# First attention of a fused decoder layer: sums from a column of ones, outputs normalised token by token

## The chip, the core and the metric

The kernel runs on one core of one Trainium2 chip. The metric is the device time of one execution in microseconds. The core has the engines PE (TensorE: matmuls and weight loads), DVE (VectorE), ACT (ScalarE), POOL (GpSimd) and SP (SyncE, which issues the transfers here). Each engine works through its own list of instructions in order; they wait for one another by semaphores.

## The reference, cut to what matters

Sixteen sequences of 512 tokens with 256 channels run through two blocks. The first is attention with 16 heads of 16 channels, whose part that is changed here reads as follows (`x` has been normalised, `q` and `k` are normalised per head):

```python
scores = jnp.einsum('nhld,nhmd->nhlm', q, k) * SM_SCALE
scores = jnp.where(causal, scores, NEG)
attn = jax.nn.softmax(scores, axis=-1)
out = jnp.einsum('nhlm,nhmd->nhld', attn, v)
out = out.transpose(0, 2, 1, 3).reshape(N, L, EMB)
return out @ Wo.T + bo
```

The second block is another causal attention with a small latent (16 heads, 32 value channels shared between the heads) and a mixture of eight experts beside a shared one. Everything is float32. Products with weights are made of three matmuls, high by high, high by low and low by high, where "high" is the operand rounded to the matmul's type fp32r and "low" the remainder (`TERMS` in the kernel).

## The kernel before

The 16 sequences ("batches") are worked on one after the other, with loops on every engine that wait for each other's signals. A batch takes some 250 us: projections and the first attention, projections and the second attention, the experts. Both attentions run through the same functions, with `a` 0 for the first and 1 for the second.

An attention has 16 units, `u`. A unit is one group of four heads, `g = u // 4`, and one tile of 128 tokens, `tile_of(u) = u % 4`. By the causal mask tile j needs keys of j+1 blocks of 128. Per unit:

1. PE makes the scores of the four heads into four PSUM banks (`score`, lines 608 and 614, the second adds the mask). The scores of unit u+1 stand in front of what PE does for unit u; each head's score waits for the exponential of the same head in the unit before.
2. DVE takes the maximum of each row, head by head (line 1055).
3. ACT makes the exponentials (line 839) into `prob` and accumulates their row sums into `sums`, which appears in the trace as an ACTIVATION_READ_ACCUMULATOR behind each one.
4. PE transposes `prob` block by block (line 625) into two PSUM banks by turns. DVE (line 1063) or ACT (line 810) copies each block to `probt`: of the ten blocks of a group ACT has the third, sixth and ninth.
5. PE multiplies the transposed blocks with the values (`weigh_values`, line 636) and adds up the output of a group in PSUM bank 6, the four heads below one another, 32 rows each, with only 16 of them filled in the first attention (`va` has zeros in the others). `weigh_values(u - 1)` stands behind the first blocks of unit u.

When a group is through, its outputs are divided by the sums: DVE takes the reciprocal (line 1067), POOL spreads it over the 32 columns of a head (`rexp`, line 459), PE transposes that (line 645) into PSUM bank 7, ACT copies bank 6 to `osb` (line 810), DVE multiplies the two to `onm` (line 1074), ACT rounds it (`oth`) and POOL, for the last group DVE, subtracts (`otl`, lines 464 and 1093). For group g this is spread over the following group: PE's transposes stand in unit 4g+4, ACT's copy and DVE's product in unit 4g+5, ACT's rounding in 4g+6. At the end of an attention PE makes the output product, for each of four token tiles over four groups of 128 rows, of which 64 are zeros in the first attention (`project_out`, line 677), and DVE adds it to the residual (line 1100).

What sets the order is the order written in each engine's `attend` function. The kernel functions that the change touches follow with their line numbers.

Of the kernel before, what the change touches and what calls it, by code (L numbers as in the profile page):

```python
# [99 lines left out]
def _build(nc, ctx, dram):  # L100
# [20 lines left out]
    woa = new("woa", [P, 2, NG, C], F32R)  # L121
# [29 lines left out]
    sums = new("sums", [P, 2, UNITS, G], F32)  # L151
    rsum = new("rsum", [P, 2, UNITS, G], F32)
# [22 lines left out]
    place[0] += 4096  # L175
    oth = at("oth", [P, NG, L], F32R, region_x)
# [33 lines left out]
    onm = new("onm", [P, L], F32)  # L210
    rexp = new("rexp", [P, NT, G, HP], F32)
# [5 lines left out]
    r_woa = new("r_woa", [P, NG, C], F32)  # L217
# [23 lines left out]
    zeroed = sem("zeroed")  # L241
# [57 lines left out]
    rsum_ready = Signal(sem("rsum_ready"), 2 * NG)  # L299
    rexp_ready = Signal(sem("rexp_ready"), 2 * NG)  # L300
    rsumt_psum = Signal(sem("rsumt_psum"), 2 * NG)
    osb_ready = Signal(sem("osb_ready"), 2 * NG)
    onm_ready = Signal(sem("onm_ready"), 2 * NG)
    oth_ready = Signal(sem("oth_ready"), 2 * NG)
    otl_ready = Signal(sem("otl_ready"), 2 * NG)
# [74 lines left out]
    def _(sp):  # L380
# [58 lines left out]
    def _(pool):  # L439
        chain = Chain(pool, pool_link, POOL_LINKS)  # L440
        nc.gpsimd.memset(r_woa[:, :, :], 0.0).then_inc(zeroed, 1)
# [4 lines left out]
        pool.wait_ge(va_zeroed, 1)  # L446

# [20 lines left out]
        def sequence(b, last):  # L468
# [26 lines left out]
            spread_sums(b, 0)  # L495

# [25 lines left out]
            spread_sums(b, 1)  # L522
# [11 lines left out]
    def _(pe):  # L534
# [14 lines left out]
        pe.wait_ge(va_zeroed, 1)  # L549
# [256 lines left out]
    def _(act):  # L806
# [25 lines left out]
        def exps(b, a, u, part):  # L832
# [474 lines left out]
```

## Time and profile before

| | us |
|---|---|
| median of 3 runs (lowest, highest) | 4082.11 (4074.95, 4089.76) |
| profiled execution | 4099.86 |
| its span, first to last instruction | 4098.0 |
| PE busy | 3508.8 (86%) |
| DVE busy | 3057.7 (75%) |
| ACT busy | 2302.6 (56%) |
| POOL busy | 805.5 (20%) |
| mean granted TensorE clock | 0.924 of 2.4 GHz |

The busy time of an engine is the time in which it works on an instruction. Every row that is shown further down has times in microseconds unless it says ns. Matmuls overlap, so the interval from one row to the next tells their pace better than their duration. A bracket at the end of a row of the timeline is the time for which the engine sat idle before it, and what released it. The granted clock is 1.00 at 2.4 GHz and 0.50 at 1.2 GHz.

### The profile page before, as it was taken

The numbers are of one execution on the slowest core, as the hardware profiler recorded it, in microseconds if no ns is written. First come the engines' busy times: TensorE is split into PE (matmuls) and PEld (weight loads), VectorE is DVE, ScalarE is ACT, GpSimd is POOL, SyncE is SP. The second block draws the span as 40 slices with busy tenths as digits, with TensorE's granted clock in tenths as the row PEclk, the third lists the DMA queues.
The fourth block names the chain that finished last, engine by engine and source line by source line (L and its number), as shares of the span: only waits on it lengthen the run. The fifth ranks groups of instructions, "written<-read, shape, count | busy, mean of one in ns | idle before, by whom it ended". The sixth has DMA issues, their size and how long they took to land.

```text
span 4098.0 us, 93072 instructions
## 1 busy us (share of the span) xinstructions
PE 3508.8 (86%) x31392; PEld 2764.5 (67%) x31392; DVE 3057.7 (75%) x6444; ACT 2302.6 (56%) x6346; POOL 805.5 (20%) x951
## 2 busy tenths in 40 slices
PE   3898888989889898897988989888898888989888
PEld 2676766767667676676766767667676766767667
DVE  3778777687777877778777687877878777787776
ACT  2655546565465654646646466554656546565464
POOL 1212222022220222202222122221212222022220
PEclk9899999999999998999989989999999999999999
DMA  3000000000000000000000000000000000000000
GB/s 73 7 2 7 7 7 7 2 7 7 7 7 2 7 7 7 7 1 12 2 7 7 7 7 2 7 7 7 7 2 7 7 7 7 2 7 7 6 2 6
DMA packets 33906, 30.35 MB, mean 7 GB/s; under 512 B 8864, under 2 KB 33312, under 8 KB 33376
## 3 DMA queue, kind: packets, MB, share of 16 engines
q1 hardware_dynamic: 33376, 23.68, 2.0%
q8 instruction: 284, 4.65, 0.5%
q14 instruction: 246, 2.02, 0.2%
HBM read 15.28 MB, written 8.39 MB: 6 GB/s over the span
## 4 chain that ended last, share of the span: by engine, by line
PE 57%; issue 14%; DVE 12%; ACT 10%; POOL 5%; SPq 1%; ACTq 0%; DVEq 0%; DMA 0%; POOLq 0%
PE bank L625 12%; PE scores L723 9%; ACT prob L839 6%; PE bank L636 6%; PE scores L612 6%; PE bank L735 4%; PE scores L613 4%; PE scores L614 3%; PE bank L596 2%; POOL qf L503 2%; PE scores L697 2%; PE scores L608 2%; PE scores L677 2%; DVE negmax L1055 1%; PE bank L555 1%
## 5 line engine op out<-in xcount | busy, mean ns | idle before, releaser
L839 ACT ACTIVATE prob<-scores,negmax 128x128 f32<-128x128 f32 (+3 forms) x2048 | 1060.7, 538 | 221.8 <-DVE negmax L1055 178.6
L1055 DVE TENSOR_REDUCE negmax<-scores 128x1 f32<-128x128 f32 (+3 forms) x2048 | 885.4, 484 | 101.0 <-PE scores L614 87.6
L625 PE MATMUL bank<-ident,prob 128*128 128x128 f32 x5120 | 730.8, 280 | 44.9 <-DVE probt L1063 35.6
L1063 DVE COPY probt<-bank 128x512 f32<-128x512 f32 x896 | 597.5, 685 | 179.2 <-PE bank L625 172.2
L625 PEld LDWEIGHTS bank<-ident,prob 128*128 128x128 f32 x5120 | 548.2, 142 | 156.0 <-DVE probt L1063 66.3
L614 PE MATMUL scores<-mask,ident 128*128 128x128 bf16 x2048 | 450.0, 231 | 0.0
L612 PE MATMUL scores<-khh,qt 128*128 128x256 f32 (+2 forms) x1024 | 438.4, 429 | 13.3 <-ACT qt L810 7.5
L839 ACT ACTIVATION_READ_ACCUMULATOR prob<-scores,negmax 128x1 f32 x2048 | 437.6, 214 | 0.0
L810 ACT ACTIVATE probt<-bank 128x512 f32<-128x512 f32 x384 | 233.0, 607 | 205.6 <-PE bank L625 205.6
L613 PE MATMUL scores<-kll,qt 128*128 128x256 f32 (+2 forms) x1024 | 345.4, 337 | 0.0
L596 PE MATMUL bank<-ident,stk 128*128 128x128 bf16 x2048 | 203.8, 286 | 153.2 <-DVE stk L1153 122.2
L723 PE MATMUL scores<-xth,wgu 128*128 128x512 f32 x1152 | 329.6, 409 | 0.0
L608 PE MATMUL scores<-qkt 96*128 96x128 bf16 (+3 forms) x1024 | 266.4, 306 | 45.9 <-DVE qkt L1043 13.9
L596 PEld LDWEIGHTS bank<-ident,stk 128*128 128x128 bf16 x2048 | 184.0, 133 | 173.2 <-issue 121.3
L614 PEld LDWEIGHTS scores<-mask,ident 128*128 128x128 bf16 x2048 | 205.2, 100 | 140.8 <-issue 110.4
L464 POOL TENSOR_TENSOR otl<-onm,oth 128x512 fp32r<-128x512 f32 x96 | 122.5, 1276 | 897.0 <-ACT oth L810 897.0
L459 POOL COPY rexp<-rsum 128x512 f32<-128x512 f32 x128 | 78.3, 612 | 856.2 <-DVE rsum L1067 856.2
L723 PEld LDWEIGHTS scores<-xth,wgu 128*128 128x128 f32 x1152 | 215.1, 195 | 44.0
L960 ACT ACTIVATE sg<-scores 128x512 f32<-128x512 f32 x144 | 86.3, 599 | 280.3 <-PE scores L723 280.3
L451 POOL TENSOR_TENSOR rstd<-var,expo 128x4 f32<-128x4 f32 x64 | 67.0, 1053 | 897.9 <-DVE var L1115 551.6
L735 PE MATMUL bank<-wd,hidh 128*128 128x256 f32 x1152 | 212.0, 281 | 27.1 <-ACT hidh L810 21.8
L612 PEld LDWEIGHTS scores<-khh,qt 128*128 128x128 f32 x1024 | 220.7, 216 | 17.7 <-ACT qt L810 9.3
(179 smaller groups left out, 6967.4 us busy)
## 6 DMA issues: line engine op xcount, KB each, us to landing
x_in<-in_x_rows SPq DMA_DIRECT2D x16, 512.0 KB, 3.5
out_rows<-x SPq DMA_DIRECT2D x16, 512.0 KB, 3.6
r_gu<-in_wg SPq DMA_DIRECT2D x2, 512.0 KB, 5.0
r_gu<-in_wu SPq DMA_DIRECT2D x2, 512.0 KB, 5.5
r_d<-in_wd SPq DMA_DIRECT2D x1, 1024.0 KB, 6.8
r_wqt<-in_wq_nope_t SPq DMA_DIRECT2D x1, 512.0 KB, 6.2
r_wqr<-in_wq SPq DMA_DIRECT2D x2, 256.0 KB, 8.8
r_wob<-in_wo SPq DMA_DIRECT2D x1, 512.0 KB, 5.3
```

What stands on the lines that cost most here:

```text
L596: ins = nc.tensor.transpose(out[:, i * P:(i + 1) * P], stk[:, t % 2, quad * 8 + i].rearrange("p s d -> p (s d)"), ident16[:, :])
L608: mm(bank[q][:, 0:n], qkt[:, h, j * P:(j + 1) * P], qkt[:, H + h, 0:n], start=True, stop=False)
L612: mm(bank[q][:, 0:m], tok, khh[:, 0:m], start=True, stop=False)
L613: mm(bank[q][:, 0:m], tok, kll[:, 0:m], start=False, stop=False)
L614: ins = mm(bank[q][:, n - P:n], ident16[:, :], mask16[:, :], start=False, stop=True)
L625: ins = nc.tensor.transpose(bank[4 + n % 2][:, q * P:(q + 1) * P], prob[:, u % 2, q, i * P:(i + 1) * P], ident[:, :])
L636: ins = mm(bank[6][q * HP:(q + 1) * HP, j * P:(j + 1) * P], val, probt[:, u % 2, i, q * P:(q + 1) * P], start=i == 0, stop=i == j)
L723: ins = mm(bank[2 * s + w][:, :], wgu[:, w_, e, k, w * I:(w + 1) * I], XT[x_][:, k], start=m == 0 and k == 0, stop=m == 2 and k == KC - 1)
L735: ins = mm(bank[4 + 2 * s + t // 2][:, (t % 2) * C:(t % 2 + 1) * C], (hidh, hidl)[x_][:, s, t * P:(t + 1) * P], wd[:, w_, e], start=m == 0 ...
L839: nc.scalar.activation(prob[:, u % 2, q, 0:n], bank[q][:, 0:n], ACT.Exp, bias=negmax[:, a, u, q:q + 1], accum_out=sums[:, a, u, q:q + 1]). ...
L1055: nc.vector.tensor_reduce(negmax[:, a, u, M * part:M * part + M], scores[:, M * part:M * part + M, 0:n], axis=AX.X, op=ALU.max, negate=Tru ...
L1063: nc.vector.tensor_copy(probt[:, u % 2, i], bank[4 + n % 2][:, :]).then_inc(probt_dve.sem, 1)
```

## The change

In the first attention only, the sum of a row of exponentials no longer comes from ACT's accumulator. The values `va` get a one in column 16 of each head's 32, so that `weigh_values` also yields the row sums, in row 16 of the head's 32 rows of bank 6. ACT copies bank 6 to `osb` as before. PE transposes `osb` (`transpose_out`), which gives 128 tokens by 128 columns per tile in bank 7. DVE takes the reciprocals of column 16 of every head and multiplies the 16 output columns by them, per token (`normalise_first`), into `otok`, where the 256 channels stand without gaps. When two groups are there, PE transposes `otok` back (`transpose_tok`), ACT rounds (`split_first`) and DVE subtracts (`low_first`), and the output product runs over two full blocks of 128 rows instead of four half-filled ones (`project_first`). POOL has no part in it any more. The output weight `woa` has two blocks instead of four and is loaded in one piece.

```diff
         nc.gpsimd.memset(va[:, :, :, :], 0.0).then_inc(va_zeroed, 1)
         pool.wait_ge(va_zeroed, 1)
+        nc.gpsimd.memset(va[:, :, :, D], 1.0).then_inc(va_zeroed, 1)
+        pool.wait_ge(va_zeroed, 2)
...
-        sp.wait_ge(zeroed, 1)
-        for q in range(G):
-            load(r_woa[q * HP:q * HP + D],
-                 dram["wo1t"].rearrange("(g q d) n -> q d g n", q=G, d=D)[q])
+        load(r_woa[:, :, :], dram["wo1t"].rearrange("(k p) n -> p k n", p=P))
...
-            spread_sums(b, 0)
...
+        def transpose_out(b, g):
+            pe.wait_ge(osb_ready.sem, osb_ready.at(b, g + 1))
             if g > 0:
-                pe.wait_ge(onm_ready.sem, onm_ready.at(b, a * NG + g))
+                pe.wait_ge(otok_ready.sem, otok_ready.at(b, g))
+            if g == NG - 2:
+                pe.wait_ge(o1l_ready.sem, o1l_ready.at(b, 1))
+            for j in range(NT):
+                ins = nc.tensor.transpose(bank[7][:, j * P:(j + 1) * P], osb[:, j * P:(j + 1) * P], ident[:, :])
+            ins.then_inc(outt_psum.sem, 1)
+
+        def transpose_tok(b, k):
+            pe.wait_ge(otok_ready.sem, otok_ready.at(b, 2 * k + 2))
+            for t in range(NT):
+                ins = nc.tensor.transpose(bank[7][:, t * P:(t + 1) * P], otok[:, t, k * P:(k + 1) * P], ident[:, :])
+            ins.then_inc(o1_psum.sem, 1)
+
+        def project_first(b, k):
+            for t in range(NT):
+                if t == 0:
+                    pe.wait_ge(o1h_ready.sem, o1h_ready.at(b, k + 1))
+                    pe.wait_ge(o1l_ready.sem, o1l_ready.at(b, k + 1))
+                for m, (x_, w_) in enumerate(TERMS):
+                    ins = mm(bank[t][:, 0:C], (o1h, o1l)[x_][:, k, t * P:(t + 1) * P], woa[:, w_, k],
+                             start=m == 0 and k == 0, stop=m == 2 and k == KC - 1)
+                if k == KC - 1:
+                    ins.then_inc(y_psum.sem, 1)
...
                 transpose_prob(b, a, u, range(early))
                 if u > 0:
                     weigh_values(b, a, u - 1)
-                    if u % NT == 0:
-                        transpose_sums(b, a, u // NT - 1)
+                    if a == 1 and u % NT == 0:
+                        transpose_sums(b, u // NT - 1)
+                    if a == 0 and u % NT == 2 and u > NT:
+                        transpose_out(b, u // NT - 1)
+                    if a == 0 and u == 3 * NT:
+                        transpose_tok(b, 0)
                 transpose_prob(b, a, u, range(early, tile_of(u) + 1))
-            transpose_sums(b, a, NG - 1)
+            if a == 1:
+                transpose_sums(b, NG - 1)
             weigh_values(b, a, UNITS - 1)
-
-            project_out(b, a, range(NG - 2))
-            project_out(b, a, range(NG - 2, NG))
...
+            if a == 0:
+                project_first(b, 0)
+                transpose_out(b, NG - 1)
+                transpose_tok(b, 1)
+                project_first(b, 1)
+            else:
+                project_out(b, range(NG - 2))
+                project_out(b, range(NG - 2, NG))
...
+                row_sums = {"accum_out": sums[:, u, q:q + 1]} if a == 1 else {}
                 nc.scalar.activation(prob[:, u % 2, q, 0:n], bank[q][:, 0:n], ACT.Exp, bias=negmax[:, a, u, q:q + 1],
-                                     accum_out=sums[:, a, u, q:q + 1]).then_inc(prob_ready.sem, 1)
+                                     **row_sums).then_inc(prob_ready.sem, 1)
...
+        def split_first(b, k):
+            act.wait_ge(o1_psum.sem, o1_psum.at(b, k + 1))
+            copy(o1h[:, k], bank[7][:, :]).then_inc(o1h_ready.sem, 1)
...
-                if u % NT == 2 and u > NT:
-                    split_out(b, a, u // NT - 1)
+                if a == 1 and u % NT == 2 and u > NT:
+                    split_out(b, u // NT - 1)
+                if a == 0 and u == 3 * NT:
+                    split_first(b, 0)
             copy_out(b, a, NG - 1)
-            split_out(b, a, NG - 1)
+            if a == 0:
+                split_first(b, 1)
+            else:
+                split_out(b, NG - 1)
...
+        def normalise_first(b, g):
+            dve.wait_ge(outt_psum.sem, outt_psum.at(b, g + 1))
+            out = bank[7].rearrange("p (t h d) -> p t h d", t=NT, h=G)
+            nc.vector.reciprocal(rs1[:, :, :], out[:, :, :, D]).then_inc(rs1_ready.sem, 1)
+            dve.wait_ge(rs1_ready.sem, rs1_ready.at(b, g + 1))
+            tt(otok[:, :, g * G * D:(g + 1) * G * D].rearrange("p t (h d) -> p t h d", h=G), out[:, :, :, 0:D],
+               rs1[:, :, :].unsqueeze(3).to_broadcast([P, NT, G, D]), ALU.mult).then_inc(otok_ready.sem, 1)
+
+        def low_first(b, k):
+            dve.wait_ge(o1h_ready.sem, o1h_ready.at(b, k + 1))
+            tt(o1l[:, k], bank[7][:, :], o1h[:, k].bitcast(F32), ALU.subtract).then_inc(o1l_ready.sem, 1)
...
-                if u > 0 and u % NT == 0:
-                    invert_sums(b, a, u // NT - 1)
+                if a == 1 and u > 0 and u % NT == 0:
+                    invert_sums(b, u // NT - 1)
                 for i in mine:
                     copy_block(b, a, u - 1, i)
-                if u % NT == 1 and u > NT:
-                    normalise_out(b, a, u // NT - 1)
-
-            normalise_out(b, a, NG - 1)
-            dve.wait_ge(oth_ready.sem, oth_ready.at(b, (a + 1) * NG))
+                if a == 1 and u % NT == 1 and u > NT:
+                    normalise_out(b, u // NT - 1)
+                if a == 0 and u % NT == 2 and u > NT:
+                    normalise_first(b, u // NT - 1)
+                if a == 0 and u == 3 * NT:
+                    low_first(b, 0)
+            if a == 0:
+                normalise_first(b, NG - 1)
+                low_first(b, 1)
+                return
```

DVE's list before, in unit 5 of the first attention (`negmax` are the maxima, `probt` a block's copy, `onm` the product with the spread reciprocals):

```order
159 L1055 TENSOR_REDUCE negmax<-scores 128x1
160 L1060 REGISTER_ALU
161 L1062 REGISTER_ALU
162 L1063 COPY probt<-bank 128x512
163 L1070 ISA
164 L1074 TENSOR_TENSOR onm<-bank,osb 128x512
165 L1054 REGISTER_ALU
166 L1055 TENSOR_REDUCE negmax<-scores 128x1
```

The product stands behind the maxima of unit 5 and in front of those of unit 6. DVE's list of the changed kernel, in unit 6, between the maxima of unit 6 and those of unit 7:

```order
169 L1108 TENSOR_REDUCE negmax<-scores 128x1
170 L1113 REGISTER_ALU
171 L1115 REGISTER_ALU
172 L1116 COPY probt<-bank 128x512
173 L1125 RECIPROCAL rs_129<-bank 128x16
174 L1127 TENSOR_TENSOR otok<-bank,rs_129 128x4x64
175 L1107 REGISTER_ALU
176 L1108 TENSOR_REDUCE negmax<-scores 128x1
```

A reciprocal and a product that read PSUM bank 7 stand there now, one unit later than the product did. PE's list of the changed kernel at the same place (the last two scores of unit 7, a block of unit 6, the values of unit 5, the transposes of `osb`, the other blocks of unit 6, a score of unit 8):

```order
163 L619 MATMUL scores<-mask_59,ident_58 128x128
164 L611 REGISTER_ALU
165 L613 MATMUL scores<-qkt 128x512
166 L619 MATMUL scores<-mask_59,ident_58 128x128
167 L628 REGISTER_ALU
168 L630 MATMUL bank<-ident,prob 128x128 x4
169 L641 MATMUL bank<-probt,va 32x128 x4
170 L638 REGISTER_ALU
171 L641 MATMUL bank<-probt,va 32x128 x4
172 L652 MATMUL bank<-ident,osb 128x128 x4
173 L630 MATMUL bank<-ident,prob 128x128 x4
174 L628 REGISTER_ALU
```

PE's list before, in unit 4, where the transposes of the spread reciprocals stood:

```order
137 L636 MATMUL bank<-probt,va 32x128 x12
138 L633 REGISTER_ALU
139 L636 MATMUL bank<-probt,va 32x128 x4
140 L645 MATMUL bank<-ident,rexp 128x128 x4
141 L606 REGISTER_ALU
142 L608 MATMUL scores<-qkt 128x384
143 L614 MATMUL scores<-mask_59,ident_58 128x128
```

PE's transposes for a group's outputs moved from unit 4g+4, in front of the scores of unit 4g+6, to unit 4g+6, behind the scores of unit 4g+7.

## Rows read from the trace of the kernel before

**Rows 1.** Page: busy us, share, instructions; and a costly group with its mean ns.
```profile
PE 3508.8 (86%) x31392; PEld 2764.5 (67%) x31392; DVE 3057.7 (75%) x6444; ACT 2302.6 (56%) x6346; POOL 805.5 (20%) x951
L839 ACT ACTIVATION_READ_ACCUMULATOR prob<-scores,negmax 128x1 f32 x2048 | 437.6, 214 | 0.0
```

**Rows 2.** Busy times by stretch: length, PE, PEld, DVE, ACT, POOL, clock, DMA, GB/s.
```profile
2156.54:2169.80 13.26, 12.31 (x160) 8.83 (x157) 11.78 (x26) 11.07 (x38) 1.88 (x2) 1.00 0.01 1
```

**Rows 3.** Timeline of DVE, units 8 to 12: start, duration, instruction, idle before.
```profile
2156.54 0.99 DVE L1055 TENSOR_REDUCE negmax<-scores 128x1 f32<-128x128 f32 x4 [0.27 <-PE scores L614]
2157.45 0.24 DVE L1067 RECIPROCAL rsum<-sums 128x16 f32<-128x16 f32 x1
2157.78 1.29 DVE L1063 COPY probt<-bank 128x512 f32<-128x512 f32 x2
2159.94 0.69 DVE L1063 COPY probt<-bank 128x512 f32<-128x512 f32 x1 [0.88 <-PE bank L625]
2160.55 1.41 DVE L1055 TENSOR_REDUCE negmax<-scores 128x1 f32<-128x256 f32 x4
2161.88 0.68 DVE L1063 COPY probt<-bank 128x512 f32<-128x512 f32 x1
2162.80 0.69 DVE L1074 TENSOR_TENSOR onm<-bank,osb 128x512 f32<-128x512 f32 x1 [0.24 <-PE bank L645]
2163.40 1.94 DVE L1055 TENSOR_REDUCE negmax<-scores 128x1 f32<-128x384 f32 x4
2165.86 2.48 DVE L1055 TENSOR_REDUCE negmax<-scores 128x1 f32<-128x512 f32 x4
2169.80 0.98 DVE L1055 TENSOR_REDUCE negmax<-scores 128x1 f32<-128x128 f32 x4 [0.27 <-PE scores L614]
```

**Rows 4.** Timeline of PE, units 8 to 11.
```profile
2161.97 0.66 PE L645 MATMUL bank<-ident,rexp 128*128 128x128 f32 x4
2164.35 1.09 PE L625 MATMUL bank<-ident,prob 128*128 128x128 f32 x8
2165.28 0.38 PE L608 MATMUL scores<-qkt 96*128 96x512 bf16 x1
...
2165.56 0.38 PE L608 MATMUL scores<-qkt 96*128 96x512 bf16 x1
...
2166.76 0.60 PE L625 MATMUL bank<-ident,prob 128*128 128x128 f32 x4
2167.30 0.65 PE L636 MATMUL bank<-probt,va 128*32 128x128 f32 x16
...
2168.99 0.66 PE L625 MATMUL bank<-ident,prob 128*128 128x128 f32 x4 [0.46 <-DVE probt L1063]
```

**Rows 5.** Timeline of DVE and PE, end of the first attention.
```profile
2188.59 0.69 DVE L1074 TENSOR_TENSOR onm<-bank,osb 128x512 f32<-128x512 f32 x1 [1.47 <-ACT osb L810]
2191.57 0.42 DVE L1100 TENSOR_TENSOR x<-scores,x_in 128x256 f32<-128x256 f32 x1 [0.90 <-PE scores L677]
2188.21 0.39 PE L677 MATMUL scores<-woa,oth 128*128 128x256 f32 x2
2188.55 0.39 PE L677 MATMUL scores<-woa,oth 128*128 128x256 f32 x2
```

**Rows 6.** As rows 2: first maxima to first reciprocal, two first and two second attentions.
```profile
1630.77:1641.32 10.55, 9.30 (x92) 5.84 (x90) 9.93 (x25) 9.70 (x37) 0.00 (x0) 1.00 0.01 2
2133.27:2144.35 11.08, 10.16 (x92) 6.62 (x91) 9.94 (x25) 9.80 (x36) 0.00 (x0) 0.85 0.01 1
2229.47:2242.98 13.51, 13.51 (x109) 10.44 (x109) 10.84 (x25) 10.95 (x39) 0.00 (x0) 0.90 0.01 2
1977.47:1992.27 14.80, 14.80 (x109) 11.59 (x109) 10.96 (x24) 11.25 (x39) 0.00 (x0) 0.81 0.01 2
```

**Rows 7.** Timeline of PE, then busy times by stretch, behind the first attention.
```profile
2196.94 1.54 PE L555 MATMUL bank<-ident,xn 128*128 128x128 f32 x8 [3.46 <-DVE xn L1166]
2200.00:2202.00 2.00, 2.00 (x6) 1.57 (x5) 0.34 (x1) 0.00 (x0) 0.00 (x0) 0.50 0.00 0
```

More of the change, by code:

```diff
@@ L120, in _build @@
     wqkv = new("wqkv", [P, 2, KC, 3 * C], F32R)
-    woa = new("woa", [P, 2, NG, C], F32R)
+    woa = new("woa", [P, 2, KC, C], F32R)
     wq2 = new("wq2", [P, 2, KC, H * DK], F32R)
@@ L150, in _build @@
     negmax = new("negmax", [P, 2, UNITS, G], F32)
-    sums = new("sums", [P, 2, UNITS, G], F32)
-    rsum = new("rsum", [P, 2, UNITS, G], F32)
+    sums = new("sums", [P, UNITS, G], F32)
+    rsum = new("rsum", [P, UNITS, G], F32)
     lg = new("lg", [P, NT, E], F32)
@@ L175, in _build @@
     place[0] += 4096
+    o1h = at("o1h", [P, KC, L], F32R, region_x)
+    o1l = at("o1l", [P, KC, L], F32R, region_x + 4096)
     oth = at("oth", [P, NG, L], F32R, region_x)
@@ L210, in _build @@
     onm = new("onm", [P, L], F32)
+    otok = new("otok", [P, NT, C], F32)
+    rs1 = new("rs1", [P, NT, G], F32)
     rexp = new("rexp", [P, NT, G, HP], F32)
@@ L216, in _build @@
     r_qkv = new("r_qkv", [P, KC, 3 * C], F32)
-    r_woa = new("r_woa", [P, NG, C], F32)
+    r_woa = new("r_woa", [P, KC, C], F32)
     r_wqt = new("r_wqt", [R, H, C], F32)
@@ L298, in _build @@
     pv_done = Signal(sem("pv_done"), 2 * UNITS)
-    rsum_ready = Signal(sem("rsum_ready"), 2 * NG)
-    rexp_ready = Signal(sem("rexp_ready"), 2 * NG)
-    rsumt_psum = Signal(sem("rsumt_psum"), 2 * NG)
+    rsum_ready = Signal(sem("rsum_ready"), NG)
+    rexp_ready = Signal(sem("rexp_ready"), NG)
+    rsumt_psum = Signal(sem("rsumt_psum"), NG)
     osb_ready = Signal(sem("osb_ready"), 2 * NG)
-    onm_ready = Signal(sem("onm_ready"), 2 * NG)
-    oth_ready = Signal(sem("oth_ready"), 2 * NG)
-    otl_ready = Signal(sem("otl_ready"), 2 * NG)
+    onm_ready = Signal(sem("onm_ready"), NG)
+    oth_ready = Signal(sem("oth_ready"), NG)
+    otl_ready = Signal(sem("otl_ready"), NG)
+    outt_psum = Signal(sem("outt_psum"), NG)
+    rs1_ready = Signal(sem("rs1_ready"), NG)
+    otok_ready = Signal(sem("otok_ready"), NG)
+    o1_psum = Signal(sem("o1_psum"), KC)
+    o1h_ready = Signal(sem("o1h_ready"), KC)
+    o1l_ready = Signal(sem("o1l_ready"), KC)
     y_psum = Signal(sem("y_psum"), 2 * NT)
@@ L548, in _ @@
         pe.wait_ge(weights_ready, len(SPLIT))
-        pe.wait_ge(va_zeroed, 1)
+        pe.wait_ge(va_zeroed, 2)
         def transpose_tokens(b, stage):
@@ L673, in project_out @@
                     if t == 0:
-                        pe.wait_ge(oth_ready.sem, oth_ready.at(b, a * NG + g + 1))
-                        pe.wait_ge(otl_ready.sem, otl_ready.at(b, a * NG + g + 1))
+                        pe.wait_ge(oth_ready.sem, oth_ready.at(b, g + 1))
+                        pe.wait_ge(otl_ready.sem, otl_ready.at(b, g + 1))
                     for m, (x_, w_) in enumerate(TERMS):
-                        ins = mm(bank[t][:, 0:C], (oth, otl)[x_][:, g, t * P:(t + 1) * P], w[:, w_, g],
+                        ins = mm(bank[t][:, 0:C], (oth, otl)[x_][:, g, t * P:(t + 1) * P], wob[:, w_, g],
                                  start=m == 0 and g == 0, stop=m == 2 and g == NG - 1)
@@ L850, in copy_out, with split_out @@
             act.wait_ge(pv_done.sem, pv_done.at(b, a * UNITS + (g + 1) * NT))
-            if g > 0:
-                act.wait_ge(onm_ready.sem, onm_ready.at(b, a * NG + g))
+            if a == 0 and g > 0:
+                act.wait_ge(outt_psum.sem, outt_psum.at(b, g))
+            if a == 1 and g > 0:
+                act.wait_ge(onm_ready.sem, onm_ready.at(b, g))
             copy(osb[:, :], bank[6][:, :]).then_inc(osb_ready.sem, 1)
-        def split_out(b, a, g):
-            act.wait_ge(onm_ready.sem, onm_ready.at(b, a * NG + g + 1))
+        def split_first(b, k):
+            act.wait_ge(o1_psum.sem, o1_psum.at(b, k + 1))
+            copy(o1h[:, k], bank[7][:, :]).then_inc(o1h_ready.sem, 1)
+        def split_out(b, g):
+            act.wait_ge(onm_ready.sem, onm_ready.at(b, g + 1))
             copy(oth[:, g], onm[:, :]).then_inc(oth_ready.sem, 1)
@@ L1063, in copy_block, with invert_sums, normalise_out @@
             nc.vector.tensor_copy(probt[:, u % 2, i], bank[4 + n % 2][:, :]).then_inc(probt_dve.sem, 1)
[L1065 to L1071 removed]
+        def invert_sums(b, g):
+            dve.wait_ge(prob_ready.sem, prob_ready.at(b, (UNITS + (g + 1) * NT) * G))
+            nc.vector.reciprocal(rsum[:, g * NT:(g + 1) * NT], sums[:, g * NT:(g + 1) * NT]).then_inc(rsum_ready.sem, 1)
+        def normalise_first(b, g):
[8 more added lines that the diff above has]
+            tt(o1l[:, k], bank[7][:, :], o1h[:, k].bitcast(F32), ALU.subtract).then_inc(o1l_ready.sem, 1)
+        def normalise_out(b, g):
+            dve.wait_ge(rsumt_psum.sem, rsumt_psum.at(b, g + 1))
+            dve.wait_ge(osb_ready.sem, osb_ready.at(b, NG + g + 1))
             if g > 0:
[L1073 removed]
+                dve.wait_ge(otl_ready.sem, otl_ready.at(b, g))
             tt(onm[:, :], bank[7][:, :], osb[:, :], ALU.mult).then_inc(onm_ready.sem, 1)
```

32 lines of the change are left out of this document (13 added, 19 removed).

## The prediction

> **What bounds the kernel now.** I read first the busy shares of the page [rows 1], then the busy times of one stretch [rows 2], then the instructions of the engines in order of time in that stretch [rows 3, 4], since an average over eight stages does not say which wait ends last in the stage that is changed. The reader is to see this. Over the span PE is busy 86% and DVE 75%. The first attention of the ninth batch runs from 2133.27 to about 2188.5 us. I take one full group of it, units 8 to 11, from the first maxima of unit 8 to the first maxima of unit 12: 13.26 us, in which DVE is busy 11.78 and PE 12.31, at full clock [rows 2]. DVE goes from one instruction to the next with waits of only 0.88, 0.24 and 0.27 us [rows 3]. DVE makes the maxima, without which ACT has no exponentials and PE no later scores; a unit cannot start before DVE has come to its maxima. So a wait on DVE in front of the maxima is the dearest thing that can be put into this loop. In the chain through the units, a late `maxima(u)` delays everything behind it one for one: from the maxima of unit 11 (2165.86) to those of unit 12 (2169.80) are 3.94 us, made of its four reductions, the copy of a block, PE's transposes that wait for this copy (0.46) [rows 4] and the score.
>
> **What goes away.** Per batch and first attention: (a) 64 of the 128 accumulator reads of ACT, half of 437.6 us in the whole program [rows 1]. ACT is not what DVE waits for [rows 3], so I give them nothing of their own; they let a unit's last exponential end 0.1 to 0.6 us sooner, which is used below. (b) DVE's reciprocal at the head of a group: 2157.45 to 2157.78, 0.33 us. (c) DVE's `onm` product with its wait, and PE's four transposes of `rexp` in front of unit 10's scores: the maxima of unit 10 follow the copy of unit 8's block instead of starting at 2163.40. (d) Pool's copies and subtractions, which are beside everything else. (e) 24 of 48 matmuls of the output product. The 48 matmuls (16 threes, one every 0.34 us) fill the end [rows 5]; eight threes fewer are 2.7 us of PE work, and the 8 transposes of `otok` put 8 x 0.13 = 1.1 us back. (f) In the preamble, one load in place of four and half a split of `woa`: about 1 us once (my estimate, the smallest term). Pool's clearing of the column of ones lies in the preamble too.
>
> **What is added, step by step (unit 10; units 6 and 14 are the same).** The order shows that DVE now has a reciprocal and a product that read PE's transposes of `osb` directly in front of the maxima of unit 11, and that PE issues these transposes only behind the scores of unit 11, a block of unit 10's transposes and all of `weigh_values(9)`. Before, the waiting product stood one unit earlier and read transposes that PE had issued a unit before. I now lay out the times, with the maxima of unit 8 at 2156.54 as before. By (b) the maxima of unit 9 start at 2160.2 (before 2160.55). By (c) the maxima of unit 10 start at 2162.15, are then paced by the exponentials of unit 9, the last of which ends at about 2163.2, and end at about 2164.0 (before 2165.3). PE: the last score of unit 10 at 2163.3, 8 transposes in 0.93 us (2164.35 to 2165.28) [rows 4], so scores of unit 11 from 2164.9; four of them at 0.28 us (2165.28 to 2165.56) to 2166.0; 4 transposes 0.54 (2166.76 to 2167.30), `weigh_values(9)` 0.57, then the four transposes of `osb`, 0.61 to their end: 2167.7. DVE has been idle since about 2165.3. It starts 0.17 us after PE's end (estimate: before, the transposes of `rexp` begun at 2161.97 with 0.66 end at 2162.63 and `onm` starts at 2162.80), needs 0.24 for the reciprocal [rows 3] and 0.42 for the product (256 elements from PSUM, as the output addition) [rows 5]. The maxima of unit 11 start at about 2168.5, where they started at 2165.86. The group therefore gets **2.6 us** longer, with the gains of (a) to (c) already in it. Three such groups: **7.8 us** a batch.
>
> **Unit 12.** `low_first(0)` on DVE waits for ACT's split, which waits for PE's transposes of `otok`, which stand behind the scores of unit 13, the transposes of unit 12 and `weigh_values(11)`. By the times of the same place a group earlier: PE ends `weigh_values` at 2161.7 and the transposes at 2162.35, ACT copies 0.6, DVE subtracts 0.65, so the maxima of unit 13 start at an equivalent of 2163.8 instead of 2160.2. ACT and PE are drained by then and give about 0.5 back in the following unit: **3.1 us**.
>
> **The end.** Before: `onm` at 2188.59, the first output addition at 2191.57 [rows 5]. After: `weigh_values(15)` ends some 1.2 us earlier (no transposes of sums, 0.5; ACT's last exponential sooner, 0.7), then comes in a row: half a product 1.36, four transposes 0.65, reciprocal and product 0.85 with the wait, four transposes 0.65, ACT's copy 0.75, DVE's subtraction 0.7, three matmuls 0.5. First addition at about 2192.0, thus **+0.4 us**. Of (e) nothing is left: PE waits in this chain. The first group, with no output work at all, gains about 0.3 by faster exponentials. Sum of waits: 7.8 + 3.1 + 0.4 - 0.3 = **11.0 us** a batch.
>
> **PE's clock.** During each new wait PE has nothing to do: in unit 10 from about 2168.2 to 2171.5, 3.3 us. In this trace a gap of 3.46 us ahead of the transposes of `xn` is followed by the level of 1.2 GHz (granted clock 0.50 at 2200 to 2202) [rows 7]. The price of the low level in this loop follows from four stretches [rows 6]. The first group took 10.55 us at clock 1.00 and 11.08 at 0.85, which is (1 - 0.85) x 2 x 11.08 = 3.3 us at half clock: 0.53 us. In the second attention, where PE has more to do, the same stretch took 13.51 us at 0.90 and 14.80 at 0.81, which is 2.7 and 5.6 us at half clock: 2.9 us more at half clock cost 1.29, or 1.5 for 3.4 us. Behind the new waits come the units richest in PE work of this loop, so I take the middle, 1.0 us for each fall, and three falls for four waits: **3.0 us** a batch. Bounds: 0 (no fall) and 4 x 6.8 x 0.45 = 12 us (every fall lasts twice as long, at the dear price).
>
> **Sum.** (11.0 + 3.0) x 16 - 1 = 223 us. On the profiled execution (span 4098.0, run 4099.86) this is 4323; the median of the runs shown is 18 us below it, so 4082 + 223 = **4305 us**, 5.5% slower. Bounds of the waits: each of the four could be 0.5 us shorter or longer by the latencies that I read from neighbours, 2 us a batch, 32 us in all. What is not shown by any row is the pace of exponentials without the read and of DVE reading PSUM with a stride; both from 0 to 0.2 us an instruction, in the 0.5.
>
> **A rule against this.** DVE has the higher share in the group than PE's weight loads: 11.78 against 8.83 of 13.26 [rows 2], while PE's own matmul rows read 12.31. The Trainium skill (Perfetto Trace Analysis, section Identifying the Most-Contended Engine) says to judge Vector by occupancy, Tensor by weight loads instead of matmul time, and to improve the engine with the highest share. By it the time follows DVE's work, which hardly changes; the trace agrees that DVE is the engine to look at, and not that its work is all that counts. That is rival 3.
>
> **Rivals.**
> 1. The waits come as worked out, the clock stays up. For it: a 1.2 GHz stretch does not appear inside any group of this trace. Against: there is no PE gap over 0.6 us in one either. 4082 + 11.0 x 16 - 1 = 4257 us.
> 2. Faster: PE is what ends last and DVE's new waits lie in DVE's spare 1.5 us per group. Then the 2.7 - 1.1 = 1.6 us of PE work decide, 4082 - 16 x 1.6 - 1 = 4055 us. It decides from the point at which DVE gets to the maxima of unit 11 no later than PE has the scores for it, under 0.3 us of wait. Against it: 2.6 us were worked out.
> 3. The waits vanish in the queues and only DVE's work counts: minus 4 `onm` (0.6 each), minus one `otl` (0.6), plus four products (0.35) and two subtractions (0.6) is -0.4 us a batch, 4075 us, within the noise.
> 4. The waits are half as long, since PE comes to the transposes sooner than I think and the clock stays up: 4082 + (4 x 1.4 + 0.1) x 16 - 1 = 4172 us.
> 5. Half clock through most of the attention: 11.0 + 12 = 23 a batch, 4449 us.
>
> **How the numbers follow.** Forecast 0.54, rival 1 0.22, rival 2 0.03, rival 3 0.03, rival 4 0.10, rival 5 0.08. A measurement of this kernel tells 0.3%, 12 us, from no change. Faster 0.03, same 0.03, slower 0.94. Range: down to 4205, which holds rival 1 with its 32 us less and about a third of rival 4; up to 4400, the forecast with twice the price of the clock (3 us x 16 = 48) and 47 us of longer waits.
>
> **What would show it.** Right: in a middle group of the first attention, DVE idle about 2.6 us in front of the reciprocal of `bank`, released by PE's transposes of `osb`, three times a batch, and once 2.5 to 3 us in front of `o1l`, released by ACT; groups of about 16 us instead of 13.25; the granted clock at 0.5 for stretches inside the attention; PE's share down. Second attention unchanged. Wrong: groups of 13 us or less, or DVE's wait at that place under 1 us; then the step "PE issues the transposes behind the scores of the next unit" was mis-read or covered.

## The result: 7.9% slower, just beyond the range

The changed kernel takes 4404.91 us (median of 4 runs, 4400.45 to 4405.51) against 4082.3 us. The ratio is 1.0788, 95% interval 1.0767 to 1.0809. The forecast was 4305 us with a range up to 4400: the direction was right, the loss, forecast at 223 us, was sized a third too small. In the profiled executions the span grows from 4098.0 to 4402.5 us, by 304.5. The busy times of the page hardly tell why: DVE works 3065.4 us where it worked 3057.7, ACT less, POOL less, PE 98 us more at a lower mean clock (0.892 where it was 0.924).

```profile
PE 3607.0 (82%) x31136; PEld 2831.7 (64%) x31136; DVE 3065.4 (70%) x6460; ACT 2207.7 (50%) x5290; POOL 699.3 (16%) x839
```

I cut every batch at DVE's first maxima and first output addition of each attention and added the pieces of all batches. The first attention goes from 926.8 to 1235.0 us (16 pieces, 57.9 to 77.2 us each), which is 308.2 of the 304.5 us. The other three stages change by -4.7, -4.6 and +9.4 us in sum, the preamble by -3.9.

DVE's timeline of the changed kernel, units 8 to 12 of the ninth batch, in the columns of [rows 3]. L1108 are the maxima, L1116 the copies, L1125 and L1127 the new reciprocal and product:

```profile
2306.09 0.93 DVE L1108 TENSOR_REDUCE negmax<-scores 128x1 f32<-128x128 f32 x4 [0.72 <-PE scores L619]
2307.67 1.46 DVE L1116 COPY probt<-bank 128x512 f32<-128x512 f32 x2 [0.65 <-PE bank L630]
2310.26 0.69 DVE L1116 COPY probt<-bank 128x512 f32<-128x512 f32 x1 [1.13 <-PE bank L630]
2310.87 1.41 DVE L1108 TENSOR_REDUCE negmax<-scores 128x1 f32<-128x256 f32 x4
2312.19 0.68 DVE L1116 COPY probt<-bank 128x512 f32<-128x512 f32 x1
2312.79 2.11 DVE L1108 TENSOR_REDUCE negmax<-scores 128x1 f32<-128x384 f32 x4
2315.27 0.69 DVE L1116 COPY probt<-bank 128x512 f32<-128x512 f32 x1 [0.37 <-PE bank L630]
2318.33 0.26 DVE L1125 RECIPROCAL rs<-bank 128x16 f32<-128x16 f32 x1 [2.37 <-PE bank L652]
2318.62 0.42 DVE L1127 TENSOR_TENSOR otok<-bank,rs 128x256 f32<-128x256 f32 x1
2318.97 2.47 DVE L1108 TENSOR_REDUCE negmax<-scores 128x1 f32<-128x512 f32 x4
2321.35 1.28 DVE L1116 COPY probt<-bank 128x512 f32<-128x512 f32 x2
2323.46 0.93 DVE L1108 TENSOR_REDUCE negmax<-scores 128x1 f32<-128x128 f32 x4 [0.82 <-PE scores L619]
```

Where DVE used to go from the copy to the maxima of unit 11 at once, it now waits 2.37 us for PE's transposes of `osb` (L652). The group takes 17.37 us instead of 13.26. But look also at the rows in front: the waits for PE's scores and blocks, 0.27 and 0.88 us in [rows 3], are now 0.72, 0.65 and 1.13. PE's timeline shows why, in the group before (unit 6; L630 are the blocks of `prob`, L641 `weigh_values`, L613 and L619 the scores):

```profile
2299.80 0.64 PE L641 MATMUL bank<-probt,va 128*32 128x128 f32 x16
2300.37 0.66 PE L652 MATMUL bank<-ident,osb 128*128 128x128 f32 x4
2300.86 0.60 PE L630 MATMUL bank<-ident,prob 128*128 128x128 f32 x4
2304.83 1.01 PE L630 MATMUL bank<-ident,prob 128*128 128x128 f32 x4 [3.36 <-DVE probt L1116]
```

PE stands for 3.36 us, where it waited 0.46 for the same copy [rows 4], and its next four transposes take 1.01 us instead of 0.66. The clock by stretch, in the columns of [rows 2]:

```profile
2300.00:2302.00 2.00, 1.47 (x24) 1.03 (x16) 0.90 (x3) 0.00 (x0) 0.00 (x0) 1.00 0.00 0
2302.00:2304.00 2.00, 0.00 (x0) 0.00 (x0) 2.00 (x4) 1.59 (x3) 0.00 (x0) 1.00 0.00 0
2304.00:2306.00 2.00, 1.17 (x8) 1.11 (x9) 1.37 (x3) 0.94 (x3) 0.00 (x0) 0.74 0.00 0
2306.00:2308.00 2.00, 2.00 (x15) 2.00 (x12) 1.26 (x5) 1.58 (x5) 0.00 (x0) 0.50 0.00 0
```

At the end of the gap PE falls to 1.2 GHz (granted clock 0.50), and what it has to do then keeps it busy without a pause, 2.00 of 2.00 us in the last row. The four groups and the whole stage of that batch, one row each:

```profile
2289.88:2306.09 16.21, 12.31 (x159) 9.25 (x157) 11.69 (x25) 9.43 (x21) 0.00 (x0) 0.97 0.01 2
2306.09:2323.46 17.37, 13.47 (x159) 10.34 (x158) 11.85 (x26) 9.40 (x21) 0.00 (x0) 0.89 0.01 1
2323.46:2341.61 18.15, 15.41 (x154) 10.80 (x152) 8.83 (x20) 7.33 (x17) 0.00 (x0) 0.76 0.01 2
2341.61:2357.31 15.70, 10.09 (x101) 7.81 (x102) 7.12 (x13) 4.87 (x8) 0.00 (x0) 0.86 0.00 1
2280.42:2357.31 76.89, 59.48 (x647) 43.31 (x645) 48.44 (x102) 38.73 (x82) 0.00 (x0) 0.88 0.01 1
```

The third row is units 12 to 14, with the lowest clock, 0.76. DVE's rows of that place and of the end, which answer to [rows 5]:

```profile
2330.88 0.69 DVE L1132 TENSOR_TENSOR o1l<-bank,o1h 128x512 fp32r<-128x512 f32 x1 [2.66 <-ACT o1h L851]
2340.97 0.26 DVE L1125 RECIPROCAL rs<-bank 128x16 f32<-128x16 f32 x1 [3.73 <-PE bank L652]
2353.36 0.26 DVE L1125 RECIPROCAL rs<-bank 128x16 f32<-128x16 f32 x1 [2.57 <-PE bank L652]
2357.31 0.42 DVE L1173 TENSOR_TENSOR x<-scores,x_in 128x256 f32<-128x256 f32 x1 [1.17 <-PE scores L667]
```

So the four waits are all there, in the places and nearly in the sizes forecast; the one of unit 14, 3.73 us here, is longer than the 2.37 of the others because PE runs at half clock in front of it (e4, at full clock, has 2.37 to 2.46 there). The half clock of this batch lies in five stretches, one behind each wait and one at the very end:

```profile
2304.98:2308.39 3.41, 3.41 (x24) 3.02 (x27) 2.01 (x6) 1.63 (x5) 0.00 (x0) 0.50 0.00 0
2322.05:2325.46 3.41, 3.37 (x20) 3.21 (x20) 1.94 (x6) 1.74 (x6) 0.00 (x0) 0.50 0.02 5
2332.28:2339.11 6.83, 6.38 (x32) 3.49 (x33) 3.84 (x8) 4.38 (x10) 0.00 (x0) 0.50 0.01 2
2345.94:2349.35 3.41, 3.24 (x33) 2.42 (x33) 1.38 (x2) 0.17 (x1) 0.00 (x0) 0.50 0.00 0
2356.18:2357.31 1.13, 1.02 (x5) 1.05 (x6) 0.00 (x0) 0.00 (x0) 0.00 (x0) 0.50 0.00 0
```

That is 17.1 us behind the four waits and 1.1 at the end, 18.2 in sum. All 16 batches have four stretches behind the waits. In two batches the stage begins at the low level, and the sum is 24.2 us. Before, it was 0, and 3.4 in three batches.

### The profile page after: what moved, and what is told of

Same layout as the page of the kernel before. It is cut to its first block, busy times and chain, and to the rows that moved or that the text cites. A ratio compares the mean times of both kernels' runs of the same rounds, so it can differ in the third digit from the quotient of the medians.

```text
span 4402.5 us, 91305 instructions
## 1 busy us (share of the span) xinstructions
PE 3607.0 (82%) x31136; PEld 2831.7 (64%) x31136; DVE 3065.4 (70%) x6460; ACT 2207.7 (50%) x5290; POOL 699.3 (16%) x839
## 4 chain that ended last, share of the span: by engine, by line
PE 62%; DVE 14%; issue 13%; POOL 5%; ACT 4%; SPq 1%; DVEq 0%; POOLq 0%; ACTq 0%; DMA 0%
PE bank L630 14%; PE scores L764 9%; PE bank L641 8%; PE scores L617 5%; PE scores L613 4%; PE bank L776 4%; PE scores L618 4%; PE scores L619 3%; DVE negmax L1108 3%; PE bank L601 2%; POOL qf L508 2%; PE scores L738 2%; PE scores L667 1%; DVE x L1309 1%; DVE res L1222 1%
## 5 line engine op out<-in xcount | busy, mean ns | idle before, releaser
L881 ACT ACTIVATE prob<-scores,negmax 128x128 f32<-128x128 f32 (+3 forms) x2048 | 991.8, 532 | 386.5 <-DVE negmax L1108 354.1
L1108 DVE TENSOR_REDUCE negmax<-scores 128x1 f32<-128x128 f32 (+3 forms) x2048 | 887.1, 485 | 106.9 <-PE scores L619 91.0
L630 PE MATMUL bank<-ident,prob 128*128 128x128 f32 x5120 | 794.2, 296 | 182.5 <-DVE probt L1116 180.1
L1116 DVE COPY probt<-bank 128x512 f32<-128x512 f32 x896 | 603.8, 688 | 273.4 <-PE bank L630 267.2
L630 PEld LDWEIGHTS bank<-ident,prob 128*128 128x128 f32 x5120 | 602.1, 151 | 295.8 <-DVE probt L1116 205.3
L619 PE MATMUL scores<-mask,ident 128*128 128x128 bf16 x2048 | 466.0, 240 | 0.0
L613 PE MATMUL scores<-qkt 96*128 96x128 bf16 (+3 forms) x1024 | 287.1, 339 | 78.6 <-ACT prob L881 64.3
L619 PEld LDWEIGHTS scores<-mask,ident 128*128 128x128 bf16 x2048 | 214.9, 105 | 141.8 <-issue 110.8
L613 PEld LDWEIGHTS scores<-qkt 96*128 96x128 bf16 x1024 | 109.8, 107 | 180.9 <-ACT prob L881 125.0
L641 PE MATMUL bank<-probt,va 128*32 128x128 f32 x5120 | 216.7, 299 | 0.0
L776 PEld LDWEIGHTS bank<-wd,hidh 128*128 128x128 f32 x1152 | 183.6, 188 | 45.3 <-ACT hidh L851 28.9
```

The lines of the kernel that those rows point to most:

```text
L613: mm(bank[q][:, 0:n], qkt[:, h, j * P:(j + 1) * P], qkt[:, H + h, 0:n], start=True, stop=False)
L619: ins = mm(bank[q][:, n - P:n], ident16[:, :], mask16[:, :], start=False, stop=True)
L630: ins = nc.tensor.transpose(bank[4 + n % 2][:, q * P:(q + 1) * P], prob[:, u % 2, q, i * P:(i + 1) * P], ident[:, :])
L641: ins = mm(bank[6][q * HP:(q + 1) * HP, j * P:(j + 1) * P], val, probt[:, u % 2, i, q * P:(q + 1) * P], start=i == 0, stop=i == j)
L776: ins = mm(bank[4 + 2 * s + t // 2][:, (t % 2) * C:(t % 2 + 1) * C], (hidh, hidl)[x_][:, s, t * P:(t + 1) * P], wd[:, w_, e], start=m == 0 ...
L1108: nc.vector.tensor_reduce(negmax[:, a, u, M * part:M * part + M], scores[:, M * part:M * part + M, 0:n], axis=AX.X, op=ALU.max, negate=Tru ...
```

## Experiments

In the table, "stage" is the first attention, the mean of 16 batches, "half clock" the time in it at 1.2 GHz, in most batches. Ratios are to the kernel before, run on the same chip.

| | us | ratio (95%) | stage | half clock |
|---|---|---|---|---|
| before | 4082.3 | 1 | 57.9 | 0 |
| changed | 4404.91 | 1.0788 (1.0767 to 1.0809) | 77.2 | 18.2 |
| e1_moved | 4082.12 | 0.9977 (0.9964 to 0.9991) | 58.1 | 0 |
| e2_norm_moved | 4166.83 | 1.0175 (1.0151 to 1.0199) | 62.0 | 3.4 |
| e3_low_moved | 4298.16 | 1.050 (1.0479 to 1.052) | 70.9 | 10.2 |
| e4_fill | 4289.81 | 1.0479 (1.0458 to 1.0499) | 70.0 | 1.0 |
| e5_end_order | 4075.73 | 0.9935 (0.9916 to 0.9953) | 57.4 | 0 |
| e6_end_halves | 4074.86 | 0.9935 (0.9917 to 0.9952) | 56.7 | 0 |
| e7_reads_back | 4127.73 | 1.0063 (1.004 to 1.0086) | 59.0 | 0.1 |
| e8_before_late | 4293.8 | 1.0467 (1.0443 to 1.0491) | 71.0 | 13.7 |
| e9_fill_groups | 4302.45 | 1.0499 (1.0473 to 1.0524) | 71.2 | 1.1 or 6.8 |
| e10_fill_one | 4352.75 | 1.0629 (1.06 to 1.0659) | 74.2 | 10.2 |

### e1: all four places moved

```diff
 # DVE
-                if a == 0 and u % NT == 2 and u > NT:
+                if a == 0 and u % NT == 3 and u > NT:
                     normalise_first(b, u // NT - 1)
-                if a == 0 and u == 3 * NT:
+                if a == 0 and u == 3 * NT + 2:
                     low_first(b, 0)
 # ACT
-                if a == 0 and u == 3 * NT:
+                if a == 0 and u == 3 * NT + 1:
                     split_first(b, 0)
```

> The changed kernel with DVE's reciprocal and product one unit later (units 7, 11, 15 instead of 6, 10, 14), ACT's split of the first block in unit 13 instead of 12 and DVE's subtraction in unit 14 instead of 12. Theory A (the whole loss comes from the place of these instructions, and from the clock that falls behind the waits they make): no wait of DVE over 1 us before them, no half clock inside the first attention beyond what the kernel before has, the stage back from 77.2 to 57 to 58 us, time 4050 to 4090 us. Theory B (the new way of normalising is dear in itself: more transposes, DVE reading PSUM with a stride, a longer end): the stage stays above 61 us, time over 4140 us.

Measured 4082.12 us, ratio 0.9977, slightly faster than the kernel before, and the stage 58.1 us: theory A. None of the four instructions waits any more in any batch. PE's list is unchanged; DVE only comes to its reciprocal a unit later, and finds the transposes done. DVE's rows at the same place:

```profile
2134.03 1.28 DVE L1116 COPY probt<-bank 128x512 f32<-128x512 f32 x2
2135.23 0.25 DVE L1125 RECIPROCAL rs<-bank 128x16 f32<-128x16 f32 x1
2135.51 0.42 DVE L1127 TENSOR_TENSOR otok<-bank,rs 128x256 f32<-128x256 f32 x1
2135.85 0.87 DVE L1108 TENSOR_REDUCE negmax<-scores 128x1 f32<-128x128 f32 x4
```

No wait in front of either. The next group takes 12.71 us where it took 13.26 [rows 2]:

```profile
2135.85:2148.56 12.71, 11.87 (x159) 8.86 (x158) 11.45 (x27) 9.52 (x21) 0.00 (x0) 1.00 0.01 2
```

This saving of 0.5 us is that of units 8 to 11 alone. By the means of 16 batches, e1 gains 0.4 us in units 0 to 3, nothing in units 4 to 7 (12.97 us, before 12.99), 0.5 in units 8 to 11 and 0.2 in units 12 to 14, 1.2 in sum. From the maxima of unit 15 to the first addition it loses 1.4 (13.9 us, before 12.5), so the stage is no shorter (below, e5).

### e2 and e3: one kind of place each

e2 has the first part of e1's diff alone, e3 the other two (with DVE's subtraction in front of its reciprocal in unit 14).

> Only the three reciprocals and products in the loop one unit later; split and subtraction of the first block stay in unit 12. Theory A: one wait of 2.7 us a batch is left, 3 to 4 us with what follows, and one fall of the clock behind it at 1.5 us: 4.5 to 5.5 us a batch over e1, so about 4130 to 4170 us. If the loss is mostly in this one place (a rival, since it drains ACT as well), the time is over 4250 us.

> Only split and subtraction of the first block moved (units 13 and 14); the three reciprocals and products stay. Theory A: three waits of 2.4 us and three falls of the clock are left, about 13 us a batch over e1, so 4290 to 4330 us. Together the gains of e2 and e3 over the changed kernel should add up to that of e1 within 30 us if each wait acts for itself; if the falls of the clock run into one another, e3 gains more than its own share and the sum is over e1's gain.

Both times fell within what was expected. Over e1's stage, e2 keeps one wait and costs 3.9 us, under the 4.5 to 5.5 expected; e3 keeps three and costs 12.8 us, 4.3 each. Together that is 16.7 us of the 19.1 between e1 and the changed kernel. The rest appears only when all four are there: behind the waits 3.4 + 10.2 = 13.6 us are at half clock apart, 17.1 together. The criterion named above, 30 us by whole times, does not tell this: the two gains over the changed kernel add up to 345 us, 22 more than e1's 323, while by the stages they are 38 us more (2.4 a batch).

### e4: the waits stay, PE is kept at work

```diff
+        def fill(b, g):
+            pe.wait_ge(otok_ready.sem, otok_ready.at(b, g + 1))
+            for n in range(12):
+                mm(bank[7][:, :], wqkv[:, 0, 0, 0:P], wqkv[:, 0, 0, 0:512], start=True, stop=True)
```

It is called in units 6, 10 and 14 in front of the last block's transposes; in unit 12 ten such matmuls go into bank 5 behind `transpose_tok`.

> The changed kernel with every wait left where it is, but PE kept at work in the four waits in the loop: 12 matmuls of 512 columns into bank 7 as soon as DVE has read it in units 6, 10 and 14, and 10 into bank 5 in unit 12; nobody reads what they write. Theory A (of the 19.3 us a batch 11 are waits and 8 the half clock): the granted clock stays at 1.00 for most of the stage, the stage falls from 77.2 to about 69 to 71 us, time 4275 to 4320 us. Rival C (the clock costs the 3 us of the forecast and the waits were sized too small): time 4350 us or more. DVE's waits before its reciprocal stay at 2.4 us in both.

Measured 4289.81 us, and the stage 70.0 us. This is the run that splits the loss. DVE's rows and the next group:

```profile
2240.45 0.26 DVE L1137 RECIPROCAL rs<-bank 128x16 f32<-128x16 f32 x1 [2.37 <-PE bank L652]
2240.74 0.42 DVE L1139 TENSOR_TENSOR otok<-bank,rs 128x256 f32<-128x256 f32 x1
2241.08 2.47 DVE L1120 TENSOR_REDUCE negmax<-scores 128x1 f32<-128x512 f32 x4
2243.47 1.28 DVE L1128 COPY probt<-bank 128x512 f32<-128x512 f32 x2
2245.02 0.88 DVE L1120 TENSOR_REDUCE negmax<-scores 128x1 f32<-128x128 f32 x4 [0.27 <-PE scores L619]
```

```profile
2245.02:2260.77 15.75, 14.85 (x172) 11.03 (x170) 11.68 (x25) 9.38 (x21) 0.00 (x0) 1.00 0.01 2
```

The same 2.37 us of wait, but behind it DVE waits 0.27 for the scores, as in the kernel before, and the group is 15.75 us long. The filling does not delay PE: the last block's transposes start 3.13 us behind the maxima of unit 7 with it and without it. The waits cost 70.0 - 57.9 = 12.1 us a batch; the clock, 77.2 - 70.0 = 7.2 us. The 1.0 us at half clock that e4 keeps at the very end of the stage counts among the 12.1: from the maxima of unit 15 on, e4 takes 0.3 us more than e1. Matmuls whose results nobody reads make the kernel 2.9% faster.

### e9 and e10: the filling in parts

e9 fills units 6, 10 and 14 only, e10 unit 12 only.

> The changed kernel with the filling matmuls of e4 only in units 6, 10 and 14; the wait of unit 12 is left empty. If every fall of the clock costs for itself at e4's average (7.1 us for 18.2 us at half clock, 0.39 us each us), one stretch of 3.4 us is left: 1.3 to 1.7 us a batch, 4310 to 4320 us. If the falls at units 12 and 14 make each other longer, the time is the same or little more, and e9 and e10 gain together more than e4 does.

> The changed kernel with the filling matmuls only in unit 12. Three gaps of 3.4 us are left, each followed by a stretch at half clock of 3.4 us if it stands alone: 10.2 us at half clock in place of 18.2, a gain of about 3 us a batch over the changed kernel, 4350 to 4365 us. If unit 12 had no share in the long stretch, the time stays at 4385 us or more.

e10's time is within what was expected, e9's 4302.45 us below the 4310 to 4320. e9's stage is 71.2 us, 6.0 below the changed kernel; e10's is 74.2, 3.0 below. Together 9.0, where e4 saves 7.2: the falls do not act each for itself. In e10 three falls of 3.4 us cost 74.2 - 70.0 = 4.2 us, 1.4 each, or 0.4 us for each us at half clock. In e9 the gap of unit 12 is followed by a fall in 9 of the 16 batches: its stages alternate between 70.1 us (1.1 at half clock, all at the very end) and 72.1 us (6.8 behind the gap, in one of the 9 only 3.4). PE's gap is the same in both kinds. Here are the first matmul behind it and the stretch that follows, in the eighth batch, whose clock stays up, and in the seventh, whose clock falls:

```profile
2006.90 0.34 PE L613 MATMUL scores<-qkt 96*128 96x384 bf16 x1 [2.33 <-ACT prob L891]
2006.90:2024.00 17.10, 15.96 (x164) 11.20 (x164) 9.95 (x20) 8.28 (x16) 0.00 (x0) 1.00 0.01 2
1743.74 0.50 PE L613 MATMUL scores<-qkt 96*128 96x384 bf16 x1 [2.33 <-ACT prob L891]
1743.48:1750.30 6.82, 6.38 (x32) 3.48 (x33) 3.84 (x8) 4.38 (x10) 0.00 (x0) 0.50 0.01 2
```

In e2, where the same gap of unit 12 is likewise the only one over 2 us, a fall follows it in all 16 batches, in 14 of them 3.4 us long:

```profile
2200.93 0.34 PE L613 MATMUL scores<-qkt 96*128 96x384 bf16 x1 [2.33 <-ACT prob L881]
2203.12:2206.53 3.41, 3.41 (x22) 2.45 (x15) 2.10 (x5) 1.99 (x5) 0.00 (x0) 0.50 0.02 5
```

So the length of a gap does not by itself decide whether the clock falls, nor for how long; what does was not tested. Unit 12's share of the clock's price is 1.1 us over e4 when the other waits are filled, and 3.0 when they are not.

### e8: the old way in the late place

```diff
 # kernel before; PE
-                    if u % NT == 0:
+                    if u % NT == (2 if a == 0 else 0) and u >= NT:
                         transpose_sums(b, a, u // NT - 1)
 # DVE
-                if u % NT == 1 and u > NT:
+                if u % NT == (2 if a == 0 else 1) and u > NT:
                     normalise_out(b, a, u // NT - 1)
```

> The kernel before, with its old way of normalising, but in the first attention PE's transposes of the spread reciprocals and DVE's product stand two and one units later, in unit 4g+6: the places that the changed kernel gives to its own. If the place alone makes the loss (theory A): DVE waits about 2.4 us in front of the product three times a batch, the groups are 15.9 us long plus 1.3 for the fall of the clock, the stage gets 11 to 13 us longer and the time is 4255 to 4290 us. If the loss needs the new way (theory B), under 4130 us.

Measured 4293.8 us, ratio 1.0467; the stage gets 13.1 us longer. Both lie a little above what was expected. DVE's rows:

```profile
2246.98 0.69 DVE L1063 COPY probt<-bank 128x512 f32<-128x512 f32 x1 [0.46 <-PE bank L625]
2250.04 0.69 DVE L1074 TENSOR_TENSOR onm<-bank,osb 128x512 f32<-128x512 f32 x1 [2.37 <-PE bank L645]
2250.65 2.47 DVE L1055 TENSOR_REDUCE negmax<-scores 128x1 f32<-128x512 f32 x4
```

The old product, put in that place, waits the same 2.37 us. Its stage of 71.0 us is that of e3 (70.9), which has the new way and the same three waits. For these three the place alone makes the loss. The wait of unit 12 has no counterpart in e8; that it too comes from the place is shown by e1 and e2. What the new way itself costs is the 1.4 us at the end of e1's stage. e8 also has a stretch of 6.8 us at half clock, in most batches behind its last gap, without a wait in unit 12.

### e5 and e6: the end, and the version that beats both

```diff
 # e1, PE, end of the first attention
-                project_first(b, 0)
+                project_first(b, 0, range(2))
                 transpose_out(b, NG - 1)
+                project_first(b, 0, range(2, NT))
                 transpose_tok(b, 1)
```

e6 also makes the last `split_first` and `low_first` in two halves, in banks 7 and 5, and PE's last product starts behind the first.

> e1 with the last four transposes of osb between the second and third token tile of the first half of the output product, instead of behind all four. ACT's copy is ready at 2166.52 in e1's trace and the transposes start at 2167.30: if the chain at the end is what costs the stage its gain (theory A), DVE's first output addition comes 0.6 to 0.7 us earlier in each batch, about 10 us in all, ratio to the kernel before about 0.995. If PE itself is the limit there (rival), nothing moves.

> e5, and the second block's split and subtraction at the end in two halves of two token tiles, in banks 7 and 5, so that PE starts the last product after the first half. Theory A: 0.4 to 0.5 us a batch more, together about 18 us below e1, ratio to the kernel before about 0.993. Rival: the fixed part of four short instructions instead of two long ones eats it; then equal to e5.

The stage falls from 58.1 to 57.4 us, as expected, and to 56.7 us, by 0.7 where 0.4 to 0.5 was expected. DVE's wait for the transposes at the end, in e1 and in e5:

```profile
2167.94 0.26 DVE L1125 RECIPROCAL rs<-bank 128x16 f32<-128x16 f32 x1 [2.57 <-PE bank L652]
```

```profile
2169.55 0.26 DVE L1126 RECIPROCAL rs<-bank 128x16 f32<-128x16 f32 x1 [1.89 <-PE bank L652]
```

The whole time follows only in part: both are 0.65% faster than the kernel before, and equal to each other, so that e6's gain over e5 is shown by the stage alone. In the profiled executions e6's first attentions are 21.5 us shorter than e1's in sum, and everything else, in which nothing differs, is 18 us longer; it is at half clock for 613 us there, in e1 for 568. Whether e5 and e6 beat e1 as whole kernels was not timed on one chip.

### e7: the accumulator reads put back

e1 with `accum_out` for both attentions.

> e1 with ACT's accumulator read back in the first attention; nobody uses the sums. Prices the removal of 1024 reads (219 us of busy time). Theory A (DVE bounds the units): 0 to 0.8 us a batch, so 0 to 13 us more than e1. Rival (ACT's pace of exponentials is what DVE and PE follow): 64 reads at 0.1 us, 6 us a batch, 100 us more.

The stage takes 59.0 us where e1 takes 58.1: 0.9 us a batch for 64 reads with 14 us of busy time, a little over theory A. The ratio moved by 0.86%, some 35 us; in the profiled executions 14.5 us of the difference lie in the first attention and 36 outside it, where both kernels have the same instructions. So the reads are worth about 15 us. Outside the first attention e7 is at half clock for 751 us, e1 for 568: the remainder goes with the clock there. Why the clock falls more often in e7's other stages was not settled.

## Why the prediction was wrong: the waits were right, the clock's price was not

- **The wait in front of the maxima of units 7, 11 and 15: right.** Forecast 2.6 us a group over 13.26, so 15.86. e4, at full clock, measured 15.75.
- **Unit 12: right.** Forecast 3.1 for it and 2.6 for unit 14, 5.7. In e4 from the maxima of unit 12 (2260.77) to those of unit 15 (2275.66) are 14.89 us; before, the like stretch was 9.31 (2169.80 to 2179.11). That is 5.6, of which 3.1 lie between the maxima of units 12 and 13.
- **"The end ... +0.4 us": mis-sized.** From the maxima of unit 15 to the first addition of the ninth batch e4 takes 14.3 us and e1 13.9, where before took 12.5: +1.8 and +1.4. I let `weigh_values(15)` end 1.2 us earlier; in e1 it ended only 0.5 earlier (8.23 us behind the maxima, before 8.72), where PE waits for block copies (0.87 and 0.17 us). The 0.7 us of it for ACT's last exponential was also more than the 0.1 to 0.6 us that (a) states. The chain behind it, forecast 5.46 us, took 5.64.
- **The waits in sum:** forecast 11.0, measured 12.1 (e4), and the end makes the difference.
- **"The middle, 1.0 us for each fall, and three falls for four waits: 3.0 us": the step that failed.** Measured 7.2. Both factors were low. There were not three stretches of 3.4 us but four, 17.1 us in sum, since the one behind unit 12 is mostly 6.8 us long; and each us cost 0.4 (e10, and 7.2 for the 17.1 here), near the second attention's 0.45 of [rows 6] and not halfway to the first group's 0.16. Why one stretch is twice as long stays open: alone, unit 12's gap is mostly followed by 3.4 us in e2 and by 0 or 6.8 in e9, and e8 has a stretch of 6.8 without it. That the price is near the second attention's because PE has hardly a pause in both (13.51 of 13.51 us in [rows 6], 17.4 of the 18.2 us at half clock here) fits the rows and is argued; no run varies PE's work at the low level. I had rival 5 at 23 us a batch with a chance of 0.08; the truth, 19.3, lies between it and the forecast.
- **(a), ACT's reads at nothing of their own:** nearly right, 0.9 us a batch (e7). **(b), (c):** e1 gains 1.2 us up to unit 15, of which 0.5 in units 8 to 11 and nothing in units 4 to 7; no run has either of them alone. **(f):** no row had the 1 us; the preamble is 3.9 us shorter, 0.1% of the time.
- **Range:** its upper end allowed twice the price of the clock for three falls, 6 us; it was 7.2, and the end added up to 1.4 more than forecast.
- **Rival 1 (clock stays up)** is what e4 brings about; it gives 4290 us there, 4257 were worked out. Rivals 2 to 4 fell. In rival 3 DVE's work alone decides: it grew from 3057.7 to 3065.4 us, 0.3%, and the time by 7.9%.

## What to carry to other kernels

Before an instruction goes into an in-order engine, look at where its releaser stands in the other engine's list: one that is issued behind the *next* unit's input makes the bound engine wait for that whole unit's work, and moving it by one unit costs nothing (e1: 0.2% faster instead of 7.9% slower). When a wait leaves PE without work, add the price of its clock at the rate of the densest stage that follows (0.4 us for each us at half clock here), count a fall for every wait, and allow for stretches twice as long as the shortest one seen.

## What the hardware showed that was not expected

- Filling PE's gaps with 46 useless matmuls a batch took 7.2 us off a stage of 77 us (e4).
- A gap of 2.33 us on PE (unit 12) was followed by a fall of the clock in 9 of 16 batches of e9 and in all 16 of e2; the three gaps of 3.36 us in all 16 batches of the changed kernel, of e3 and of e10.
- Stages with the same instructions differ in sum between kernels: what lies outside the first attention takes 18 us more in e6 than in e1 and 36 us more in e7, with 45 and 182 us more at half clock. A change of under 0.5% in this kernel is better judged by its stage than by its time.
